# First work of three attentions placed in the stages ahead of them, in a four-layer transformer kernel

## What is computed

```python
# layer 0, and once more inside the MLP of layer 1: causal, 16 heads of width 16
scores = where(causal, q @ k.T / 4, -big); out = softmax(scores) @ v @ Wo
# layer 1: 32 query heads, 8 key heads of width 64, a mask of 64 keys around each
# query, and a learned sink `s` for each head in the softmax denominator
# layer 2: "state" attention, 16 heads of width 128 and 64 slots
s = clip(hs @ Ws1.T @ Ws2.T + bs2, -32, 32)
es, enz = exp(s), exp(-cumlogsumexp(s))
ok = enz * (tril(q @ k.T * scale) @ es);  qv = softmax(ok)
o = tril((qv * enz) @ es.T) @ v;  out = (rmsnorm(o) * silu(g)) @ Wo.T
```

## Time and profile before

| what | value |
|---|---|
| median of 3 runs | 2832.79 us (2831.49 to 2838.64) |
| the profiled execution's own time | 2839.57 us |
| its span, first to last instruction | 2837.9 us |
| PE / DVE / ACT / POOL busy | 90% / 57% / 44% / 45% |
| window attention, its first DMA to its last product | 631.96 to 1375.13 us |
| state attention, its first DMA to its last matmul | 1838.78 to 2345.88 us |

### The profile page before, as it was taken

How to read it: one execution, slowest core, us unless ns; L and a number is a source line. 1 busy time by engine, 2 the same in 40 slices (tenths; PEclk the granted TensorE clock), 3 DMA queues, 4 the chain that set the end, 5 groups by cost and what they waited for, 6 DMA issues and landing times. The chain is left out here.

```text
span 2837.9 us, 40914 instructions
## 1 busy us (share of the span) xinstructions
PE 2542.1 (90%) x14498; PEld 1689.7 (60%) x14498; DVE 1628.5 (57%) x2144; ACT 1260.2 (44%) x2154; POOL 1281.4 (45%) x1118
## 2 busy tenths in 40 slices
PE   6887999876999999999878878889999988998798
PEld 4443777653444444444564436668888876776676
DVE  4663555566666667664236533377777645555555
ACT  4464332452555555555334652245655642333232
POOL 4001344464888888888521003255454533442243
PEclk9788999896999999999987978889999997999799
DMA  1000111112111011010000001010000001110011
GB/s 50 1 1 22 34 50 45 45 62 57 30 24 38 23 38 38 16 31 1 26 20 1 1 6 43 29 42 26 20 31 20 20 5 35 50 44 21 26 43 43
DMA packets 40141, 82.16 MB, mean 29 GB/s; under 512 B 7856, under 2 KB 21424, under 8 KB 39472
## 3 DMA queue, kind: packets, MB, share of 16 engines
q1 hardware_dynamic: 39696, 79.94, 10.0%
q10 hardware_dynamic: 288, 0.13, 0.0%
HBM read 60.12 MB, written 3.15 MB: 22 GB/s over the span
## 5 line engine op out<-in xcount | busy, mean ns | idle before, releaser
L1937 DVE TENSOR_REDUCE a1h_mseg<-bank 128x2 f32<-128x1024 f32 x256 | 302.4, 1222 | 185.3 <-PE bank L1702 177.2
L1864 ACT ACTIVATE a1h_prob<-bank 128x512 f32<-128x512 f32 x440 | 247.0, 598 | 191.5 <-PE bank L1758 105.2
L1686 POOL TENSOR_TENSOR a_qk<-a_qk,a1h_prob 128x512 f32<-128x512 f32 x230 | 298.2, 1328 | 49.0 <-ACT a1h_prob L1864 49.0
L63 POOL TENSOR_TENSOR f_wh<-f_raw,ones_r 128x768 fp32r<-128x768 f32 (+1 forms) x74 | 111.8, 1511 | 407.3 <-PE bank L464 367.6
L453 PE MATMUL bank<-x_norm_h,f_wh 128*128 128x512 f32 x592 | 244.1, 412 | 6.6 <-PEq L3057 2.5
L453 PE MATMUL bank<-x_norm_l,f_wh 128*128 128x512 f32 x592 | 238.7, 403 | 0.0
L453 PE MATMUL bank<-x_norm_h,f_wl 128*128 128x512 f32 x592 | 237.7, 401 | 0.0
L656 DVE SCALAR_TENSOR_TENSOR f_tf<-bank,f_bias,f_sg 128x512 f32<-128x512 f32 x148 | 111.0, 751 | 191.8 <-PE bank L453 185.4
L1771 PE MATMUL bank<-a1h_prob,a_v 128*64 128x512 f32 x880 | 215.0, 603 | 0.0
L1756 PE MATMUL bank<-a1h_ql,a1h_k 128*128 128x512 f32 x512 | 202.1, 395 | 0.0
L544 ACT ACTIVATE f_hhi<-f_hf 128x512 fp32r<-128x512 f32 x124 | 78.3, 632 | 276.3 <-DVE f_hf L664 276.3
(11 more groups left out here) (583 smaller groups left out, 6153.4 us busy)
## 6 DMA issues: line engine op xcount, KB each, us to landing
f_raw<-in_l_w_dram SPq DMA_DIRECT2D x66, 385.0 KB, 3.0
a1h_st_q<-a_qk SPq DMA_DIRECT2D x128, 128.0 KB, 2.3
a_qk<-l_keys SPq DMA_DIRECT2D x32, 128.0 KB, 2.7
l2a_qkraw<-in_l2a_wqk_dram SPq DMA_DIRECT2D x32, 128.0 KB, 2.1
l2a_vraw<-in_l2a_wvg_dram SPq DMA_DIRECT2D x8, 512.0 KB, 3.9
f_raw<-in_l_w_dram SPq DMA_DIRECT2D x8, 449.0 KB, 3.3
a1p_raw<-in_l1a_w_dram SPq DMA_DIRECT2D x20, 128.0 KB, 2.0
l_keys<-a_qk SPq DMA_DIRECT2D x4, 512.0 KB, 4.0
```

Source lines behind the costliest of these rows:

```text
L63: return pool.tensor_tensor(dst, src, one.to_broadcast(list(src.shape)), ALU.mult)
L1686: pool.tensor_tensor(out, first, slot_of[t % NP], ALU.add).then_inc(sum_done, 1)
L1864: act.activation(slot_of[t % NP], core.bank[2 + t % 3][:, :], ACT.Exp, scale=scale).then_inc(p_ready, 1)
L1937: dve.tensor_reduce(mseg[:, :, qb, s], spare(("A", n, k))[:, :, :], AX.X, ALU.max).then_inc(a_read, 1)
```

## The change

Each attention now calls the stage in front of it, and the output product calls the attention, each with its first work as arguments; tiles are allocated earlier for it.

- Small attentions: `put` is cleared and all six `put` writes are made by POOL in the normalisation, ahead of the weight splits. At the end of `project` ACT makes the first two high parts, DVE the low part of chunk 0 (ahead of the emptying of the value banks), POOL the low part of chunk 1, then `mpos`, masks and the negated identity. The eight warming matmuls (L1375) are gone.
- Window attention: the keys' own block is gone. In `project` SP loads masks, the queries of batch 0 and, when chunk 16 is written, the first keys by eight DMAs from SBUF to SBUF, and writes chunks 17 to 19 to device memory. POOL makes the constants at its end; DVE splits the first keys between the rotary turn and the emptying of the value banks. In the attention's block the head has only the 8 segments of query blocks 0 to 3; the other 8 stand in steps 0 and 1 of batch 0, their maxima enter by a second `max_rows` ("N") at step 2, and the 16 segments of batch 1 stand 0, 0, 3, 3, 4, 4, 2, 0 in the steps of batch 0. The low parts of batch 0's queries go from DVE to POOL.
- Output products: weights are loaded and split while the attention runs. The zero matmuls are gone (`start` and `stop` are given at the first and last chunk), splits and products go half by half, and the first half of the additions stands before the last matmuls end. The zero bias is gone.
- State attention: first loads and splits stand in the normalisation. The prologue is written out; it holds pair 0's values and gates. The reciprocals of pair 0 stand in iteration 0, behind `add_states`.

```diff
 def project(..., before, fill=None, added=None, sync=None, gpsimd=None, scalar=None, vector=None):
+        def written(eng, c):
+            eng.wait_ge(out_done, 2 * c + 10)
...
         @block.vector
...
                 chunks(dve, turn)
+            if vector is not None:
+                vector(dve, written)
             if v_bias is not None:
                 dve.wait_ge(vb_in, 16)
             for t in range(TB):
                 dve.wait_ge(v_ready, t + 1)
...
 def attend_causal(...):
+        def first_high(act, written):
+            for c in range(2):
+                written(act, c)
+                high(act, c)
+        def first_low(dve, written):
+            low(dve, 0, lo[0])
+        def constants(pool):
+            pool.memset(put[:, :, :, :].bitcast(F32), 0.0).then_inc(made, 1)
...
+        def masks(pool, written):
+            low(pool, 1, lo_again)
+            pool.memset(mpos[:, :, :, :].bitcast(F32), 0.0).then_inc(made, 1)
+            pool.wait_ge(c_in, 16)
+            pool.tensor_copy(mk[:, :, :], mk_raw[:, :, :]).then_inc(made, 1)
+            pool.tensor_scalar(nident[:, :], core.ident[:, :], -1.0, None, ALU.mult).then_inc(made, 1)
+        before(constants, sync=masks_in, gpsimd=masks, scalar=first_high, vector=first_low)
...
-            for x in range(4):
-                pe.matmul(core.bank[5][:, :], core.ident[:, :], qk[:, 0, half(x % 2)], start=True, stop=True)
-            pe.wait_ge(made, 3)
...
+            others(head)
...
 def attend_window(...):
+    HEAD = ((0, 1), (3, 4), (6, 7), (8, 9))
+    LATE = (((2,), (5,), (10, 11)), ((12, 13), (14, 15)))
...
+        def first_in(sp, written):
...
+            written(sp, 0)
+            for a in range(PER):
+                load_queries(sp, 0, a)
+            written(sp, NQ)
+            for a in range(PER):
+                for r in range(4):
+                    r0 = 64 * (r % 2) + 32 * a
+                    sp.dma_start(core.xn[32 * r:32 * r + 32, a, :], qk[r0:r0 + 32, NQ, :]).then_inc(k0_in[a], 16)
...
+        def first_keys(dve, written):
+            for a in range(PER):
+                dve.wait_ge(k0_in[a], 64)
+                dst, st = kn[:, 0, a, :], core.xn[:, a, :]
+                dve.tensor_copy(dst, st).then_inc(kn_steps, 1)
+                dve.wait_ge(kn_steps, 2 * a + 1)
+                dve.tensor_tensor(dst[MR[a]], st[MR[a]], dst[MR[a]].bitcast(F32), ALU.subtract).then_inc(kn_steps, 1)
...
-            pe.wait_ge(prep, 7)
-            for x, size in enumerate(VISITS):
-                visit(0, range(sum(VISITS[:x]), sum(VISITS[:x + 1])))
+            for ks in HEAD:
+                visit(0, ks)
             max_rows(0)
...
+                        if n == 0 and j < 2:
+                            for ks in LATE[j]:
+                                visit(0, ks)
+                        if n == 0 and j == 2:
+                            max_rows(0, "N")
...
 def out_product(...):
+        before(sync=first_loads, gpsimd=first_splits)
...
+            for h in range(NH):
+                dve.wait_ge(y_half, h + 1)
+                for m in range(DC):
...
 def state_attention(...):
+            project(0, 0, 0)
+            project(0, 0, 1)
+            project(0, 1, 0)
+            project(0, 1, 1)
+            slot_scores(0)
+            values(0, 0)
+            project(0, 2, 0)
+            values(0, 1)
+            project(0, 2, 1)
+            project(0, 3, 0)
+            values(0, 2)
+            project(0, 3, 1)
+            values(0, 3)
...
                 add_states("s1", s1, s1_added, p, 0)
                 add_states("s1", s1, s1_added, p, 1)
+                if not p:
+                    invert(0, 0)
+                    invert(0, 1)
+                    invert(1, 0)
+                invert(p + 1, 1)
...
                 normalise(p, 0)
```

More of the change, by code:

```diff
@@ L1412, in rounding @@
                     act.activation(dst, src, ACT.Identity, bias=one_row[:, :]).then_inc(rounded, 1)
-            high(0)
-            high(1)
-            act.wait_ge(cleared, 1)
-            columns = core.ident[:, :].rearrange("p (n v u) -> p v u n", v=4, u=2)
-            for kind, places in enumerate(PLACES[2:4]):
-                rows = put[:, 2 + kind, :, :].rearrange("p v (u n) -> p v u n", u=2)
-                for s in places:
-                    act.activation(rows[:, :, :, 16 * s:16 * s + 16], columns, ACT.Copy).then_inc(keys_made, 1)
-            act.wait_ge(made, 4)
             for kind, i, *c in head:
@@ L1842, in _, with first_queries_high @@
         def _(act):
+            def first_queries_high():
+                for h in range(NH):
+                    for a in range(PER):
+                        act.wait_ge(q_in[a], 64)
+                        act.activation(QA[0][:, a, half(h)], st_q[:, a, half(h)], ACT.Copy).then_inc(q_hi, 1)
             def queries_high(n):
@@ L1937, in maxima, with blocks, row_maxima @@
                 dve.tensor_reduce(mseg[:, :, qb, s], spare(("A", n, k))[:, :, :], AX.X, ALU.max).then_inc(a_read, 1)
-            def row_maxima(n):
-                dve.wait_ge(a_read, len(SEGS) * (n + 1))
+            def blocks(n, kind):
+                return slice(0, TB) if n else slice(0, TB // NH) if kind == "M" else slice(TB // NH, TB)
+            def row_maxima(n, kind="M"):
+                b = blocks(n, kind)
+                count = b.stop - b.start
+                dve.wait_ge(a_read, len(SEGS) * (n + 1) if n or kind == "N" else sum(len(g) for g in HEAD))
@@ L2078, in _, with product @@
                                                  ALU.add).then_inc(added, 1)
+                    elif add_x:
+                        dve.tensor_tensor(dst[:, m, half(h)], dst[:, m, half(h)], ps, ALU.add).then_inc(added, 1)
                     else:
-                        dve.tensor_scalar(dst[:, m, half(h)], ps, bc[:, m:m + 1], None, ALU.add).then_inc(added, 1)
+                        dve.tensor_copy(dst[:, m, half(h)], ps).then_inc(added, 1)
         @block.tensor
         def _(pe):
-            for m in range(DC):
+            def product(c, i, slot):
+                w_slot = c % SLOTS if isinstance(c, int) else slot
+                pe.wait_ge(w_split, c * 2 + 2)
+                begin, end = isinstance(c, int) and c == 0, isinstance(c, int) and c == n_chunks - 1
@@ new lines, in product @@
+                    for m in range(DC):
+                        for n, (w, x) in enumerate(((wh, oh), (wl, oh), (wh, ol))):
+                            mm = pe.matmul(core.bank[DC * h + m][:, :], w[:, w_slot, m * P:(m + 1) * P],
+                                           x[:, slot, half(h)], start=begin and n == 0, stop=end and n == 2,
+                                           skip_group_check=True)
+                    if end:
+                        mm.then_inc(y_half, 1)
+                if not end:
+                    mm.then_inc(y_done, 1)
@@ L2607, in _ @@
             split_vg_high(0)
-            for p in range(-1, len(PAIRS) + 1):
+            swap(0, 0, 0)
+            swap(0, 0, 1)
+            swap(0, 1, 0)
+            swap(0, 1, 1)
+            exp_slots(0)
+            swap(0, 2, 0)
+            copy_values(0, 0)
+            gates(0, 0)
+            swap(0, 2, 1)
+            swap(0, 3, 0)
+            copy_values(0, 1)
+            gates(0, 1)
+            swap(0, 3, 1)
+            copy_values(0, 2)
+            gates(0, 2)
+            copy_values(0, 3)
+            gates(0, 3)
+            for p in range(len(PAIRS) + 1):
                 copy_slots(p, 0)
@@ L3030, in layer1_attention, with attended @@
-        out_product(nc, core, "a1o", qk, 16, a["l1a_wo"], a["zero_cols"], core.x, True)
+        v_room = nc.sbuf_tensor("a1_v", [P, TB, 8, 64], F32)
+        keys = nc.dram_tensor("l1_keys", (4, P, T), F32).ap()
+        normed = lambda **ahead: norm(nc, core, "n1a", core.x, True, core.eps5, room=qk[:, 0:2 * DC, :], **ahead)
+        def attended(**ahead):
+            with v_room as v:
+                projected = lambda **more: project(nc, core, "a1p", 20, a["l1a_w"], a["l1a_tab"], qk, None, a["l1a_wv"],
+                                                   None, v, 8, 64, normed, **more)
+                attend_window(nc, core, "a1h", qk, keys, v, 0.125, 4, a["spread"], a["window"], a["l1a_sink"], projected,
+                              **ahead)
```

581 lines of the change are left out of this document (319 added, 262 removed).

## The result

The changed kernel takes 2788.0 us (median of 4 runs, 2783.61 to 2794.26) against 2832.84 for the one before (4 runs, 2831.49 to 2838.64): a ratio of 0.9826, 95% interval 0.981 to 0.9843, so 44.8 us or 1.7% faster. The prediction said 2787, with 2770 to 2802 as its range. The profiled execution took 2794.26 us, 45.3 less than that of before.

What follows compares the result with a forecast made beforehand. TensorE, busy 90% of the span, was taken as the bound, with time to win only at the seams. Terms 22.5 + 4.4 + 15 + 3.5 = 45.4 us off the 2832.79 median give 2787.4; range 2770 to 2802.

Steps and rivals of the forecast that it cites:

- Term 1, front: Front of the window attention: without the keys' own block, score tiles start at 646.9 against 678.39, gaining 31.5 us.
- The exclusion: DVE's first key split in `project`: DVE and POOL shut each other out of SBUF, costing 2 us, bounds 0 and 3.9.
- Term 1, batch 0: Window attention, batch 0: eight more segments, in steps 0 and 1, give back 9.0 us, bounds 4.2 and 13.
- Term 2: Fronts of the two causal attentions: placement starts earlier, 1.8 us in layer 0 and 2.6 in layer 1; 4.4, bounds 2.5 to 6.1.
- if first, DVE's value copies and PE's tiles slip and the block ends at 49.4: Layer 0's end of `project`, if POOL's low part precedes DVE's: block ends at 49.4 (before: 46.1), placement still gaining 1.8 us.
- Term 3: Three output products: first product 3.6 us earlier, additions 1.35 us less, 5.0 each; 15 us together, bounds 13 to 16.5.
- Term 4: State attention: prologue gains 1.7 us and pair 0 gains 2; 3.5 us after rounding down, bounds -2 and 6.
- 48 more matmuls (11.3 us) that fit into PE's gaps: State attention's prologue: the added matmuls fill PE's idle gaps, so the prologue takes 30.2 us against 31.9.
- B: Seams close better: no DVE-POOL exclusion, no clock lost in `project`, batch 0 pays only PE's 4.2; 2776 us, chance 0.17.
- C: DVE bounds the moved work: batch 0 at 13, exclusion 3.9, clock 4.6, state attention -2; 2801 us, chance 0.16.
- D: Window attention's first keys land 10 us after DVE is ready, costing some 13 us; 2800 us, chance 0.06.
- E: PE's clock stays at 1.2 GHz after the window attention's head, through full batches; 2833 us and more, chance 0.03.

## Why the prediction was right, and where it was not

The sum of the terms was 45.4 and they measured 45.4. That it fits to a tenth is luck: the four terms are off by +0.6, -2.3, +1.5 and +0.2 us, which cancel, and inside term 1 an error of 3.0 stands against one of 2.4, on stages that stray by as much. What was right is the mechanism: the seams give the time, and each but layer 0's front gave about what was forecast.

- **Term 1, front, 31.5: measured 34.5.** Keys on time, value tiles waiting for DVE, half clock behind PE's stop: all there. Sizes: first key split to block 8.4 predicted and some 5.5 measured (the last turn to the next block 13.7 against 8.1 before). The exclusion cost 0.25 on the second copy and nothing on the subtractions, in place of 2; GpSimd's own constants took 1.94 and 2.19 (1.49 and 1.33 in the kernel before, with DVE idle), so it was mostly GpSimd that waited. PE's stop was 4.27, for the 6 forecast. The head, 13.4 predicted, took 13.3.
- **Term 1, batch 0, 9.0: measured 11.2** for the batch and 11.4 to the last key sums. The step was right in kind (PE waits for DVE's reductions in steps 0 and 1), but I had the bursts in steps 0 and 1 end some 3 us after PE's work, and step 1 alone is 5.4 longer than before, at a clock of 0.69 in place of 1.00.
- **Term 2, 4.4: measured 2.1**, below its bound of 2.5. Layer 1's MLP gave 2.9 for 2.6. Layer 0 gave -0.8 for +1.8, a loss for a gain: its step "if first, DVE's value copies and PE's tiles slip and the block ends at 49.4" left out the clock. GpSimd went first, DVE's low part took 3.40, and behind PE's stop of 5.64 us the four value tiles were 1.28 us apart in place of 0.68, 2.4 us. I had priced just this in term 1 and not here.
- **Term 3, 15: measured 16.5**, at its upper bound (17.4 with the later cut in layer 1). Start 3.5 for 3.6 and additions 1.5 for 1.35, as the run that undid them confirms. The rest is in layer 1's 16 chunks, where PE's own stretch fell from 48.7 to 46.5; I had no term for it.
- **Term 4, 3.5: measured 3.7** (1.0 and 2.7 for 1.7 and 2.0). The sum was right by errors that cancel: the step "48 more matmuls (11.3 us) that fit into PE's gaps" is wrong, they are all on the path, 11.0 us, against 12.0 that the rest of the new prologue gained (19.9 without them, 31.9 before). The four reciprocals in a row took 6.4 us that were free to take; PE's stop behind them was 6.9, for the 9 forecast.
- **Rivals.** B (seams close better) held for the exclusion in layer 1 only; of C, batch 0 came half of the way (11.2, between 9.0 and 13); D and E did not happen.

The Trainium skill, page "SBUF — State Buffer", section "Who interferes with whom", says that a DVE instruction with two inputs in SBUF (or a copy in a two-port mode) and a GpSimd instruction that reads SBUF exclude each other for a whole instruction, whichever starts first. By that rule layer 0's low part had to take 2.3 + 1.2; the trace agrees (3.40, a little of it side by side), and the splits of 4.11 and 4.23 were drawn out in the same way. The keys of layer 1 don't agree: DVE's first copy began 0.80 us into GpSimd's first constant and still took 0.68, the next copy 0.93, and each subtraction 1.22, although each of the four began while a constant was under way, as far as GpSimd's rough spans tell. There the measurement decides, and not the order of starting.

## What to carry to other kernels

Work moved into the stage in front is not free where it stands ahead of what frees PE's banks: put it behind as many bank copies as there are banks (4.1 us less at each of two fronts here, of which the whole kernel didn't clearly show its part), and look in the timeline whether GpSimd is in an instruction on SBUF at the same time. Long instructions in a row on one engine (here four reciprocals) are to be broken up over the idle times that the profile shows ahead of them; that gave more than the new prologue did. And a gain in one stage is read between fixed events of the trace, with a second execution of the same kernel beside it, since stages without an edit moved by as much as some of the terms.

## What the runs showed of the hardware that I had not expected

- The same code comes out at one of two lengths from one execution to the next: 35.1 or 39.0 us for the attention of layer 3 with its normalisation, 15.2 to 15.6 or 17.9 for the first normalisation, with the granted clock lower in the longer one (0.76 against 0.85, and 0.75 against 0.82 below) and the busy time of DVE, ACT and POOL within 0.2 us. Windows of the first normalisation, in the changed kernel and in the one with the late output weights:

```profile
8.03:25.98 17.95, 13.12 (x48) 8.97 (x48) 7.68 (x12) 6.62 (x12) 12.93 (x15) 0.75 0.32 110
```

```profile
8.02:23.26 15.24, 10.30 (x48) 6.75 (x48) 7.58 (x12) 6.73 (x12) 12.92 (x15) 0.82 0.39 129
```

- Even DVE instructions of 128x8 get longer beside GpSimd: 0.81 and 1.19 us in place of 0.17, each ending within 0.02 us of a GpSimd sum.
- A GpSimd constant took 2.19 us in place of 1.33 beside DVE's subtraction of 1.22, which was not longer for it: in one place GpSimd waited, in another DVE.
